# A two-layer CIN recommender tower on one core: the contraction goes by halves of a chunk's rows, as 64-column tiles, and the dense layers move to pairs 4 to 6

## The chip, the cores and the metric

The kernel runs on one core of one Trainium2 chip. The metric is the device time of one execution in microseconds; the median of several runs counts.

## What is computed

For each of 512 samples 32 rows of 64 numbers are gathered from 32 tables by index. Two layers of a compressed interaction network follow, then three dense layers. All is float32.

```python
def _cin_layer(X, prev_x, W, b):
    bsz, m, d = X.shape
    h = prev_x.shape[1]
    x_i = jnp.einsum('bmd,bhd->bmhd', X, prev_x).reshape(bsz, m * h, d)
    x_i = jnp.einsum('oc,bcd->bod', W, x_i) + b[None, :, None]
    return x_i
...
for W, b in ((W0, b0), (W1, b1)):
    x_i = _cin_layer(X, prev_x, W, b)
    cin_outs.append(x_i.sum(axis=2))
    prev_x = x_i
...
z = jnp.concatenate(cin_outs, axis=1)
h = jnp.concatenate([z, dense_ctx], axis=1)
h = jnp.maximum(h @ W_top1 + b_top1, 0.0)
h = jnp.maximum(h @ W_top2 + b_top2, 0.0)
y = h @ W_top3
```

W0 is 128 x 1024, W1 is 128 x 4096, W_top1 is 272 x 512, W_top2 is 512 x 256, W_top3 is 256 x 1.

## The kernel before

Only the sums of a layer's output over the 64 dimensions are wanted. So the kernel never forms the second layer: it computes, for each sample, the third-order moments of its fields (sum over d of x_i x_j x_m), and contracts them with coefficients that it first works out from W0 and W1.

**Setup.** W1 is multiplied with the pairs of W0 (L573, 64 matmuls), the results are folded and transposed (L595, 69 transposes), and the coefficients DT lie in the tile `coef`: 69 slots of 128 x 128. Eight more slots, W0Z, serve the first layer's output.

**Chunks.** The samples go in four chunks (c = 0 to 3) of 128. A chunk's rows are two halves h of 64 samples, one on partitions 0 to 63 and one on 64 to 127, where a partition is a dimension d. Sample numbers b within a half run from 0 to 63. A chunk has eight pairs (j = 0 to 7) of two steps each (k), and a step takes four values of b.

- *Gathers.* GpSimd gathers the rows of one field at a time (L269, 32 per chunk, eight to a group g) into XG. The gathers of group g of a chunk wait until TensorE has transposed that group of the chunk before.
- *x_group(c, g)* (L551): TensorE transposes eight fields, four transposes of 128 x 128 (L558). ScalarE and VectorE copy the result to XT, in the program order of each. Group 3 of the next chunk (its last) is transposed at the boundary between two chunks, the others behind pairs 1, 3 and 6 (chunk 0) or 1, 3 and 5.
- *products(c, j)* on VectorE (L370): PP, the products of two fields, for the eight values of b of a pair. ScalarE first copies XT to PSUM (x_copy) and fills two columns of PP (e_columns). PP has two buffers.
- *moments(c, k)* on TensorE (L598): 32 matmuls of 64 rows, 32 weight columns and 80 moving columns (L613). The trace shows a float32 matmul as two records, each a weight load (PEld) and a matmul (PE), so a step has 64 records and a pair 128. The outputs lie in two PSUM banks of the four 0 to 3.
- *moments_out(c, k)* on ScalarE (L480): one copy of 128 x 640 from those banks to U, which has two buffers, one for even and one for odd chunks. It adds one to the semaphore u_ev.
- *contract(c)* on TensorE (L618), a Python generator that emits one matmul, here called a tile, at each next(): 8 tiles with W0Z (L627), then 69 with DT (L632). The weights are 128 x 128, and the moving side is 128 columns of U, a whole chunk. They sum up in PSUM bank 6 as z0 and z1. It waits for u_ev of all sixteen steps of its chunk, and for z_ev, the eviction of the chunk before from bank 6. A chunk's 77 tiles are spread over the next chunk as filler between its moments: AHEAD tiles before the x_group at the boundary, BEHIND behind it, BETWEEN between the two steps of pair 0, and TILES[c][j] behind pair j. Chunk 3's stand alone at the end.
- *z_out(c)* on ScalarE (L491) evicts z0 and z1 to ZT in pair 5 of the next chunk. *layers* on TensorE (L659) and *layer_out* on ScalarE (L497) are the dense layers of the chunk before: h1 (L639, L644, L645) behind pair 6, h2 (L650) behind pair 7, y (L656) behind the boundary. They share banks 4 and 5 with the x_groups, in turns that `bank_uses` (L71) writes down.

Each engine works off its list in program order, and the order is written out by hand. The tables that set it on TensorE:

```python
XPAIR = ({1: 0, 3: 1, 6: 2}, {1: 0, 3: 1, 5: 2}, {1: 0, 3: 1, 5: 2}, {})
TILES = {1: (10, 6, 5, 5, 5, 5), 2: (14, 9, 9, 8, 8, 8), 3: (15, 9, 9, 9, 9, 9)}
AHEAD, BEHIND, BETWEEN = (26, 6, 2), 12, 3
LAYER = {6: "h1", 7: "h2"}
```

The loop over chunks and pairs stands at L679 and behind.

Of the kernel before, what the change touches and what calls it, by code (L numbers as in the profile page):

```python
# [18 lines left out]

# [1 line left out]

# [6 lines left out]
P = 128  # L30
NC = B // P
# [4 lines left out]
BW = HF + 4  # L36
# [3 lines left out]
TB = HF + 1  # L40
NT = NBK // NQ * TB
NN = NT + 1
BP = P // 2
KB = 4
NK = BP // KB
NJ = NK // 2
# [15 lines left out]
RESTS = (2, 4, 6)  # L62
WARM = 10
XPAIR = ({1: 0, 3: 1, 6: 2}, {1: 0, 3: 1, 5: 2}, {1: 0, 3: 1, 5: 2}, {})
TILES = {1: (10, 6, 5, 5, 5, 5), 2: (14, 9, 9, 8, 8, 8), 3: (15, 9, 9, 9, 9, 9)}
AHEAD, BEHIND, BETWEEN = (26, 6, 2), 12, 3
XFIELDS = F // NG
LAYER = {6: "h1", 7: "h2"}


def bank_uses():  # L71


    uses = [(("x", 0, g), 4 + g % 2) for g in range(NG)]
    later = []
    for c in range(NC):
        for j in range(NJ):
            if c and j in LAYER:
                later.append((LAYER[j], c - 1, 0))
            if j in XPAIR[c]:  # L80
                later.append(("x", c + 1, XPAIR[c][j]))
        if c < NC - 1:
            later.append(("x", c + 1, NG - 1))
        if c:
            later.append(("y", c - 1, 0))
    return uses + [(use, 4 + i % 2) for i, use in enumerate(later)]


def build(nc, ids, tables, near_a, near_b, cross_a, cross_b, w1t, w0z, b0, b1, ctxt, wt1, bt1, wt2, bt2, wt3, out):
# [3 lines left out]
    with ExitStack() as ctx:  # L93
        def sb(name, shape, dt=f32):
            return ctx.enter_context(nc.sbuf_tensor(name, shape, dt))
# [14 lines left out]
        U = main[:, U_AT:MAIN_N].rearrange("p (c n h b) -> p c n h b", c=2, h=2, b=BP)  # L110
# [9 lines left out]
        DT = coef[:, :].rearrange("p (n o) -> p n o", o=H)  # L120
# [9 lines left out]
        W0Z = sb("W0Z", [P, 8, H])  # L130
# [13 lines left out]
        bank = [psum[:, i, :] for i in range(8)]  # L144
# [21 lines left out]
        t_mm, u_ev = sem("t_mm"), sem("u_ev")  # L166
# [7 lines left out]
        for use, to in pair_uses:  # L174
            pair_bank[use] = to
            if use[0] == "x":
                _, c, g = use
# [235 lines left out]
        def _(act):  # L413
# [83 lines left out]
            def layer_out(c, layer):  # L497


                src = bank[pair_bank[layer, c, 0]]  # L500
                if layer == "h1":
                    act.wait_ge(h1_mm, 4 * (c + 1))
                    for k in range(4):
                        last = a.activation(H1[:, k, :], src[:, k * P:k * P + P], ACT.Relu, bias=bt1s[:, k:k + 1])
                elif layer == "h2":
                    act.wait_ge(h2_mm, 2 * (c + 1))
                    for n in range(2):
                        last = a.activation(H2[:, n, :], src[:, n * P:n * P + P], ACT.Relu, bias=bt2s[:, n:n + 1])
                else:
                    act.wait_ge(y_mm, c + 1)  # L510
                    last = copy(Y[:, P * c:P * c + P], src[0:1, 0:P])
                last.then_inc(pair_act, 1)

            for c in range(NC):
                for j in range(NJ):
                    moments_out(c, 2 * j)
                    moments_out(c, 2 * j + 1)
                    if j < NJ - 2:
                        x_copy(NJ * c + j + 2)
                        e_columns(NJ * c + j + 2)  # L520
                    if c and j in LAYER:
                        layer_out(c - 1, LAYER[j])
                    if c and j == 5:
                        z_out(c - 1)
                    if j in XPAIR[c]:
                        x_out(act, copy, c + 1, XPAIR[c][j], 0).then_inc(x_act, 1)
                if c < NC - 1:
                    last_group(c + 1)
                if c:
                    layer_out(c - 1, "y")  # L530
            z_out(NC - 1)

            for k in (0, 2):
# [9 lines left out]
        def _(pe):  # L543
            mm, transpose = nc.tensor.matmul, nc.tensor.transpose
# [39 lines left out]
            for i, n in enumerate(DORDER):  # L584
# [9 lines left out]
                for k in range(min(4, NN - 4 * n)):  # L594
                    last = transpose(bank[i % 4][:, k * P:(k + 1) * P], D[:, 4 * n + k].rearrange("p q m -> p (q m)"), ident[:, :])  # L595
# [19 lines left out]
                                      pp[:, :, q * 2 * BW:(q + 1) * 2 * BW], start=True, stop=True)  # L615
                last.then_inc(t_mm, 1)

            def contract(c):  # L618

                if c:  # L620
                    pe.wait_ge(z_ev, 2 * c)
                z1, z0 = bank[6][:, 0:P], bank[6][:, P:2 * P]
                pe.wait_ge(u_ev, NK * (c + 1))
                if c == 0:
                    pe.wait_ge(w0z_in, 16)
                for n in range(8):
                    mm(z0, W0Z[:, n, :], U[:, c % 2, n // 2 * BW + TB + n % 2].rearrange("p h b -> p (h b)"),  # L627
                       start=n == 0, stop=n == 7)
                    yield
                for n in range(NN):  # L630
                    at = n // TB * BW + n % TB if n < NT else BW - 1
                    last = mm(z1, DT[:, n, :], U[:, c % 2, at].rearrange("p h b -> p (h b)"), start=n == 0, stop=n == NN - 1)  # L632
                    if n == NN - 1:
                        last.then_inc(z_mm, 1)
                    yield

# [22 lines left out]
            def layers(c, layer):  # L659


                to = bank[pair_bank[layer, c, 0]]
                wait_out(pe, pair_before[layer, c, 0])
                if layer == "h1":
                    pe.wait_ge(z_ev, 2 * (c + 1))
                    pe.wait_ge(mlp_in, 64)
                    for k in range(4):
                        context(c, k, to[:, k * P:k * P + P])
                        layer_1(k, to[:, k * P:k * P + P])
                elif layer == "h2":  # L670
                    wait_out(pe, ("h1", c, 0))
                    for n in range(2):
                        layer_2(n, to[:, n * P:n * P + P])
                else:
                    wait_out(pe, ("h2", c, 0))
                    layer_3(to[0:1, 0:P])

            tiles = iter(())
            for c in range(NC):  # L679
                for j in range(NJ):  # L680
                    moments(c, 2 * j)
                    if c and j == 0:
                        for _ in range(BETWEEN):
                            next(tiles)
                    moments(c, 2 * j + 1)
                    for _ in range(TILES[c][j] if c and j < len(TILES[c]) else 0):
                        next(tiles)
                    if c and j in LAYER:
                        layers(c - 1, LAYER[j])
                    if j in XPAIR[c]:  # L690
                        x_group(c + 1, XPAIR[c][j])
                tiles = contract(c)
                if c < NC - 1:
                    for _ in range(AHEAD[c]):
                        next(tiles)
                if c < NC - 1:
                    x_group(c + 1, NG - 1)
                    for _ in range(BEHIND):
                        next(tiles)
                if c:  # L700
                    layers(c - 1, "y")
            for _ in tiles:
                pass

# [52 lines left out]
```

## Time and profile before

| what | us |
|---|---|
| median of three runs (363.14 to 365.93) | 365.27 |
| the profiled execution | 361.78 |
| its span, first to last instruction | 360.0 |
| TensorE matmuls busy | 260.7 |
| ScalarE / VectorE / GpSimd busy | 132.8 / 123.4 / 123.4 |
| mean granted TensorE clock, as a share of full speed | 0.796 |

Times within the execution count from the span's start. PE is TensorE's matmuls, PEld its weight loads, DVE VectorE, ACT ScalarE, POOL GpSimd. A row with "[0.93 <-issue]" says that the engine was idle for 0.93 us before it and that no wait seen in the trace explains it. "x18" counts records. The granted clock is given as a share of full speed, where 1.00 is 2.4 GHz and 0.50 is 1.2 GHz. In a merged row the time runs from the first record's start; some matmul records can be missing from a count.

### The profile page before, as it was taken

The numbers are of one execution on the slowest core, as the hardware profiler recorded it, in microseconds if no ns is written. First come the engines' busy times: TensorE is split into PE (matmuls) and PEld (weight loads), VectorE is DVE, ScalarE is ACT, GpSimd is POOL, SyncE is SP. The second block draws the span as 40 slices with busy tenths as digits, with TensorE's granted clock in tenths as the row PEclk, the third lists the DMA queues.
The fourth block names the chain that finished last, engine by engine and source line by source line (L and its number), as shares of the span: only waits on it lengthen the run. The fifth ranks groups of instructions, "written<-read, shape, count | busy, mean of one in ns | idle before, by whom it ended". The sixth has DMA issues, their size and how long they took to land.

```text
span 360.0 us, 11320 instructions
## 1 busy us (share of the span) xinstructions
PE 260.7 (72%) x5169; PEld 209.8 (58%) x5169; DVE 123.4 (34%) x243; ACT 132.8 (37%) x287; POOL 123.4 (34%) x134
## 2 busy tenths in 40 slices
PE   8654177957365647559594848768598999989997
PEld 7321055746142515348392727557397898978896
DVE  1000028282724334204351423306166728652001
ACT  4421156756432405203040403414055655645002
POOL 5777626377526270623507070524400000000000
PEclk9855559899558565859587765959699999999999
DMA  6911101011001010100101010000000000000000
GB/s 193 330 26 26 26 4 28 7 23 28 21 14 22 13 27 7 20 11 9 22 4 27 6 26 7 19 16 11 20 4 4 5 4 4 5 5 4 2 0 2
DMA packets 8657, 9.27 MB, mean 26 GB/s; under 512 B 4225, under 2 KB 5121, under 8 KB 8610
## 3 DMA queue, kind: packets, MB, share of 16 engines
q0 software_dynamic: 4096, 4.20, 5.8%
q1 hardware_dynamic: 3650, 4.34, 3.8%
q8 instruction: 41, 0.67, 0.8%
q10 hardware_dynamic: 864, 0.01, 0.1%
q14 instruction: 6, 0.05, 0.1%
HBM read 8.54 MB, written 0.00 MB: 24 GB/s over the span
## 4 chain that ended last, share of the span: by engine, by line
PE 69%; issue 20%; another core or an unknown queue 4%; ACT 4%; DVE 3%; POOL 0%; POOLq 0%; DVEq 0%; ACTq 0%
PE psum L613 24%; PE psum L632 20%; PE psum L573 11%; PE psum L627 3%; ACT main L417 2%; PE psum L650 2%; DVE PP L384 2%; PE psum L558 2%; PE psum L595 2%; PE psum L549 1%; PE psum L639 1%; PE psum L644 1%; PE psum L645 1%; ACT coef L417 1%
## 5 line engine op out<-in xcount | busy, mean ns | idle before, releaser
L269 POOL DMA_INDIRECT XG<-in_tbl,idx x128 | 122.7, 959 | 132.3 <-PE psum L558 90.3
L417 ACT ACTIVATE main<-psum 128x640 f32<-128x640 f32 (+4 forms) x146 | 80.0, 565 | 164.0 <-PE psum L613 96.2
L613 PE MATMUL psum<-PP,main 64*32 64x80 f32 x4096 | 95.3, 265 | 61.5 <-issue 52.9
L613 PEld LDWEIGHTS psum<-PP,main 64*32 64x32 f32 x4096 | 65.9, 118 | 87.3 <-issue 75.3
L384 DVE TENSOR_TENSOR PP<-psum,main 128x1024 f32<-128x1024 f32 (+1 forms) x72 | 76.2, 1101 | 90.5 <-ACT psum L417 90.1
L632 PE MATMUL psum<-main,coef 128*128 128x128 f32 x552 | 73.0, 290 | 1.9 <-issue 1.9
L632 PEld LDWEIGHTS psum<-main,coef 128*128 128x128 f32 x552 | 68.1, 202 | 7.1 <-issue 5.4
L573 PE MATMUL psum<-main 128*128 128x256 f32 (+1 forms) x128 | 42.9, 480 | 25.0 <-issue 16.3
L573 PEld LDWEIGHTS psum<-main 128*128 128x128 f32 x128 | 26.8, 227 | 40.1 <-issue 26.6
L417 ACT ACTIVATE coef<-psum 128x256 f32<-128x256 f32 (+2 forms) x43 | 20.3, 541 | 17.3 <-PE psum L573 7.6
L197 DVE COPY main<-psum 64x256 f32<-64x256 f32 (+1 forms) x26 | 9.3, 356 | 49.1 <-PE psum L558 45.2
L221 DVE COPY main<-psum 128x276 f32<-128x276 f32 x4 | 2.5, 631 | 41.6 <-remote 37.9
L317 DVE TENSOR_TENSOR main<-main,coef 128x128 f32<-128x128 f32 (+8 forms) x73 | 14.1, 263 | 3.4 <-issue 1.5
L417 ACT ACTIVATE PP<-main 128x256 f32<-128x256 f32 x32 | 14.7, 459 | 0.2
L417 ACT ACTIVATE psum<-main 128x256 f32<-128x256 f32 x32 | 12.3, 385 | 5.1 <-DVE PP L388 4.8
L388 DVE TENSOR_TENSOR PP<-psum,main 128x128 f32<-128x128 f32 (+1 forms) x36 | 13.8, 383 | 0.0
L595 PE MATMUL psum<-ident,main 128*128 128x128 f32 x69 | 8.8, 279 | 4.3 <-issue 2.0
L627 PE MATMUL psum<-main,W0Z 128*128 128x128 f32 x64 | 10.2, 319 | 2.0 <-ACT main L417 2.0
L558 PE MATMUL psum<-ident,XG 128*128 128x128 f32 x64 | 11.1, 302 | 0.0
L627 PEld LDWEIGHTS psum<-main,W0Z 128*128 128x128 f32 x64 | 9.5, 232 | 2.5 <-ACT main L417 2.3
L595 PEld LDWEIGHTS psum<-ident,main 128*128 128x128 f32 x69 | 7.4, 140 | 5.5 <-issue 2.7
L407 DVE TENSOR_SCALAR H<-psum,bt1s 128x128 f32<-128x128 f32 x2 | 0.7, 351 | 28.2 <-PE psum L645 28.2
(44 smaller groups left out, 95.8 us busy)
## 6 DMA issues: line engine op xcount, KB each, us to landing
main<-in_w1t SPq DMA_DIRECT2D x8, 256.0 KB
XG<-in_tbl,idx POOLq DMA_INDIRECT x128
WT<-in_wt SPq DMA_DIRECT2D x2, 512.0 KB
W0Z<-in_w0z SPq DMA_DIRECT2D x1, 512.0 KB
main<-in_near_a SPq DMA_DIRECT2D x1, 136.0 KB
main<-in_near_b SPq DMA_DIRECT2D x1, 136.0 KB
main<-in_cross_a SPq DMA_DIRECT2D x1, 128.0 KB
main<-in_cross_b SPq DMA_DIRECT2D x1, 128.0 KB
```

The lines of the kernel that those rows point to most:

```text
L197: last = copy(XT[rows, c % 2, b0:b1, at:at + XFIELDS - 1:2], src[:, BP * h + b0:BP * h + b1, :])
L269: pool.indirect_dma_start(out=XG[:, f, :], out_offset=None, in_=tables[f], in_offset=bass.IndirectOffsetOnAxis(ap=idx[:, c, f:f + 1], axis=0),
L317: last = v.tensor_tensor(d, d, in_fx(off, [[NX + HF, j1 - j0], [1, HF]]), ALU.add)
L384: v.tensor_tensor(pp[:, lo:lo + nb, g * NS:(g + 1) * NS, 0:HF], in_xp(lo * F + g * HF, [[F, nb], [0, NS], [1, HF]]), in_main(at, [[2 * XW, ...
L388: v.tensor_tensor(pp[:, lo:lo + nb, :, HF].rearrange("p b (g m) -> p b g m", g=2), XP[:, lo:lo + nb, :].rearrange("p b (g m) -> p b g m", ...
L417: return a.activation(dst, src, ACT.Copy)
L558: last = transpose(bank[pair_bank[use]][:, i * P:(i + 1) * P], XG[:, f:f + 2, :].rearrange("p f d -> p (f d)"), ident[:, :])
L573: mm(bank[n % 4][:, 0:pairs.shape[1]], W1T[:, m, :], pairs, start=True, stop=True).then_inc(v_mm, 1)
L595: last = transpose(bank[i % 4][:, k * P:(k + 1) * P], D[:, 4 * n + k].rearrange("p q m -> p (q m)"), ident[:, :])
L613: last = mm(bank[2 * (n % 2) + h][F * q:F * q + F, i * CW:i * CW + CW], XT[lo:lo + BP, c % 2, KB * k + i, NS:NS + F], pp[:, :, q * 2 * BW: ...
L627: mm(z0, W0Z[:, n, :], U[:, c % 2, n // 2 * BW + TB + n % 2].rearrange("p h b -> p (h b)"), start=n == 0, stop=n == 7)
L632: last = mm(z1, DT[:, n, :], U[:, c % 2, at].rearrange("p h b -> p (h b)"), start=n == 0, stop=n == NN - 1)
```

## The change

The contraction of a chunk goes by halves of the values of b. `contract(c, half)` takes as its moving side the 32 values of b of its half, in both h: 64 columns in place of 128, with the same weights. It writes the matching 64 columns of z0 and z1. Each half has its 77 tiles, and a chunk's two halves follow each other in one chain, which begins behind the moments of pair 4 (FROM) of the chunk itself. The first half waits for u_ev of eight steps, the second for all sixteen. Only the last tile of the second half signals z_mm.

The tables are new: TILES has an entry for all chunks and pairs, the x_group at a boundary has 26 tiles ahead of it after chunk 0 and none after chunks 1 and 2, and 24 behind it; 6 stand between the steps of pair 0. z_out moves from pair 5 to pair 3, h1 from 6 to 4, h2 from 7 to 5, and y from the boundary to pair 6, on TensorE and on ScalarE. Whatever of the chain is left after the last pair of chunk 3 is emitted at the end as before.

```diff
@@ -62,10 +63,12 @@
 RESTS = (2, 4, 6)
 WARM = 10
 XPAIR = ({1: 0, 3: 1, 6: 2}, {1: 0, 3: 1, 5: 2}, {1: 0, 3: 1, 5: 2}, {})
-TILES = {1: (10, 6, 5, 5, 5, 5), 2: (14, 9, 9, 8, 8, 8), 3: (15, 9, 9, 9, 9, 9)}
-AHEAD, BEHIND, BETWEEN = (26, 6, 2), 12, 3
+FROM = NJ // 2
+TILES = ((0, 0, 0, 0, 19, 19, 19, 20), (12, 3, 3, 3, 10, 12, 17, 19),
+         (20, 16, 15, 15, 10, 12, 17, 19), (20, 16, 15, 15, 19, 19, 19, 20))
+AHEAD, BEHIND, BETWEEN = (26, 0, 0), 24, 6
 XFIELDS = F // NG
-LAYER = {6: "h1", 7: "h2"}
+LAYER = {4: "h1", 5: "h2", 6: "y"}
 
 
 def bank_uses():
@@ -81,8 +84,6 @@
                 later.append(("x", c + 1, XPAIR[c][j]))
         if c < NC - 1:
             later.append(("x", c + 1, NG - 1))
-        if c:
-            later.append(("y", c - 1, 0))
     return uses + [(use, 4 + i % 2) for i, use in enumerate(later)]
 
 
@@ -520,14 +521,12 @@
                         e_columns(NJ * c + j + 2)
                     if c and j in LAYER:
                         layer_out(c - 1, LAYER[j])
-                    if c and j == 5:
+                    if c and j == FROM - 1:
                         z_out(c - 1)
                     if j in XPAIR[c]:
                         x_out(act, copy, c + 1, XPAIR[c][j], 0).then_inc(x_act, 1)
                 if c < NC - 1:
                     last_group(c + 1)
-                if c:
-                    layer_out(c - 1, "y")
             z_out(NC - 1)
 
             for k in (0, 2):
@@ -615,22 +614,22 @@
                                       pp[:, :, q * 2 * BW:(q + 1) * 2 * BW], start=True, stop=True)
                 last.then_inc(t_mm, 1)
 
-            def contract(c):
-
-                if c:
+            def contract(c, half):
+
+                if c and half == 0:
                     pe.wait_ge(z_ev, 2 * c)
-                z1, z0 = bank[6][:, 0:P], bank[6][:, P:2 * P]
-                pe.wait_ge(u_ev, NK * (c + 1))
-                if c == 0:
+                rows = slice(half * BP // 2, (half + 1) * BP // 2)
+                z1, z0 = [bank[6][:, at:at + P].rearrange("p (h b) -> p h b", h=2)[:, :, rows] for at in (0, P)]
+                pe.wait_ge(u_ev, NK * c + NK // 2 * (half + 1))
+                if c == 0 and half == 0:
                     pe.wait_ge(w0z_in, 16)
                 for n in range(8):
-                    mm(z0, W0Z[:, n, :], U[:, c % 2, n // 2 * BW + TB + n % 2].rearrange("p h b -> p (h b)"),
-                       start=n == 0, stop=n == 7)
+                    mm(z0, W0Z[:, n, :], U[:, c % 2, n // 2 * BW + TB + n % 2, :, rows], start=n == 0, stop=n == 7)
                     yield
                 for n in range(NN):
                     at = n // TB * BW + n % TB if n < NT else BW - 1
-                    last = mm(z1, DT[:, n, :], U[:, c % 2, at].rearrange("p h b -> p (h b)"), start=n == 0, stop=n == NN - 1)
-                    if n == NN - 1:
+                    last = mm(z1, DT[:, n, :], U[:, c % 2, at, :, rows], start=n == 0, stop=n == NN - 1)
+                    if half and n == NN - 1:
                         last.then_inc(z_mm, 1)
                     yield
 
@@ -675,7 +674,6 @@
                     wait_out(pe, ("h2", c, 0))
                     layer_3(to[0:1, 0:P])
 
-            tiles = iter(())
             for c in range(NC):
                 for j in range(NJ):
                     moments(c, 2 * j)
@@ -683,22 +681,20 @@
                         for _ in range(BETWEEN):
                             next(tiles)
                     moments(c, 2 * j + 1)
-                    for _ in range(TILES[c][j] if c and j < len(TILES[c]) else 0):
+                    if j == FROM:
+                        tiles = itertools.chain(contract(c, 0), contract(c, 1))
+                    for _ in range(TILES[c][j]):
                         next(tiles)
                     if c and j in LAYER:
                         layers(c - 1, LAYER[j])
                     if j in XPAIR[c]:
                         x_group(c + 1, XPAIR[c][j])
-                tiles = contract(c)
                 if c < NC - 1:
                     for _ in range(AHEAD[c]):
                         next(tiles)
-                if c < NC - 1:
                     x_group(c + 1, NG - 1)
                     for _ in range(BEHIND):
                         next(tiles)
-                if c:
-                    layers(c - 1, "y")
             for _ in tiles:
                 pass
```

TensorE, chunk 0 from pair 4 to pair 0 of chunk 1. L613 is moments (64 matmuls a pair), L627 and L632 the tiles, L558 an x_group. Before:

```order
L613 MATMUL psum<-PP,main 32x80 x192
L558 MATMUL psum<-ident,XG 128x128 x4
L613 MATMUL psum<-PP,main 32x80 x64
L627 MATMUL psum<-main,W0Z 128x128 x8
L632 MATMUL psum<-main,coef 128x128 x18
L558 MATMUL psum<-ident,XG 128x128 x4
L632 MATMUL psum<-main,coef 128x128 x12
L613 MATMUL psum<-PP,main 32x80 x32
L632 MATMUL psum<-main,coef 128x128 x3
```

The same stretch now, where the lines are one or more lower (L612 moments, L631 the tiles with DT, L557 an x_group):

```order
L612 MATMUL psum<-PP,main 32x80 x64
L627 MATMUL psum<-main,W0Z 128x2x32 x8
L631 MATMUL psum<-main,coef 128x2x32 x11
L612 MATMUL psum<-PP,main 32x80 x64
L631 MATMUL psum<-main,coef 128x2x32 x19
L612 MATMUL psum<-PP,main 32x80 x64
L631 MATMUL psum<-main,coef 128x2x32 x19
L557 MATMUL psum<-ident,XG 128x128 x4
L612 MATMUL psum<-PP,main 32x80 x64
L631 MATMUL psum<-main,coef 128x2x32 x20
L627 MATMUL psum<-main,W0Z 128x2x32 x8
L631 MATMUL psum<-main,coef 128x2x32 x18
```

The first half's 77 tiles stand in pairs 4 to 7 of chunk 0 itself, and the 26 behind them belong to the second half.

TensorE at the end of chunk 3, from the moments of pair 7 on. Before (L650 is h2 and L656 y of chunk 2, L639 the first matmuls of chunk 3's h1):

```order
L613 MATMUL psum<-PP,main 32x80 x64
L650 MATMUL psum<-H,WT 128x128 x8
L656 MATMUL psum<-H,wt3s 1x128 x2
L627 MATMUL psum<-main,W0Z 128x128 x8
L632 MATMUL psum<-main,coef 128x128 x69
L639 MATMUL psum<-CTX,WT1C 128x128 x4
```

Now, from the tiles of pair 5 on (L649 is h2, L655 y, L638 the context part of h1):

```order
L631 MATMUL psum<-main,coef 128x2x32 x19
L649 MATMUL psum<-H,WT 128x128 x8
L612 MATMUL psum<-PP,main 32x80 x64
L631 MATMUL psum<-main,coef 128x2x32 x19
L655 MATMUL psum<-H,wt3s 1x128 x2
L612 MATMUL psum<-PP,main 32x80 x64
L631 MATMUL psum<-main,coef 128x2x32 x20
L627 MATMUL psum<-main,W0Z 128x2x32 x8
L631 MATMUL psum<-main,coef 128x2x32 x69
L638 MATMUL psum<-CTX,WT1C 128x128 x4
```

The end still has 77 tiles, now of half the columns; h2 and y have left it.

## Rows read from the trace of the kernel before

**Rows 1.** The page: engine, busy us, share, records; and the chain by engine

```profile
PE 260.7 (72%) x5169; PEld 209.8 (58%) x5169; DVE 123.4 (34%) x243; ACT 132.8 (37%) x287; POOL 123.4 (34%) x134
...
PE 69%; issue 20%; another core or an unknown queue 4%; ACT 4%; DVE 3%; POOL 0%; POOLq 0%; DVEq 0%; ACTq 0%
```

**Rows 2.** Windows: us, busy us (records) by engine, clock, DMA share, GB/s

```profile
126.84:136.90 10.06, 4.48 (x36) 1.99 (x36) 2.63 (x5) 0.01 (x1) 6.57 (x7) 0.56 0.15 28
136.90:144.18 7.28, 5.67 (x298) 5.03 (x298) 4.47 (x5) 4.83 (x9) 0.00 (x0) 0.50 0.02 5
158.40:166.25 7.85, 7.85 (x54) 7.85 (x55) 0.00 (x0) 0.00 (x0) 0.00 (x0) 0.76 0.00 0
218.55:225.22 6.67, 6.67 (x160) 6.06 (x167) 3.42 (x4) 3.83 (x9) 0.00 (x0) 0.62 0.01 2
258.26:292.12 33.86, 32.56 (x1115) 29.59 (x1115) 18.68 (x24) 18.18 (x39) 0.00 (x0) 0.96 0.02 4
298.21:331.67 33.46, 31.66 (x1174) 29.03 (x1175) 19.91 (x24) 16.72 (x36) 0.00 (x0) 1.00 0.02 4
305.93:309.66 3.73, 3.73 (x147) 3.49 (x147) 2.61 (x3) 2.00 (x4) 0.00 (x0) 1.00 0.03 7
337.11:352.52 15.41, 15.41 (x140) 15.41 (x140) 0.00 (x0) 0.00 (x0) 0.00 (x0) 1.00 0.00 1
```

**Rows 3.** GpSimd and TensorE in chunk 0, timelines: start, us, what, [idle before]

```profile
125.55 0.94 POOL L269 DMA_INDIRECT XG<-in_tbl,idx  x1 [6.73 <-PE psum L558]
...
129.76 0.49 PE L613 MATMUL psum<-PP,main 64*32 64x80 f32 x4 [0.93 <-issue]
...
136.90 3.34 PE L613 MATMUL psum<-PP,main 64*32 64x80 f32 x170 [0.23 <-issue]
141.84 2.41 PE L613 MATMUL psum<-PP,main 64*32 64x80 f32 x128 [1.60 <-DVE PP L388]
```

**Rows 4.** The chain in chunk 3, one pair: start, us, what

```profile
305.93 2.21 PE psum L632 x18
308.13 1.53 PE psum L613 x115
```

**Rows 5.** The chain behind the last moments: start, us, what

```profile
333.76 0.63 ACT H L508 x2
...
334.53 0.60 PE psum L656 x4
335.12 1.98 PE psum L627 x16
337.11 15.41 PE psum L632 x138
```

**Rows 6.** Weight loads singly (start, us), then by line (duration ns min/median/max)

```profile
331.67 0.19 PEld L650 LDWEIGHTS psum<-H,WT 128*128 128x128 f32 x1
331.67 0.30 PEld L650 LDWEIGHTS psum<-H,WT 128*128 128x128 f32 x2
...
357.51 0.09 PEld L656 LDWEIGHTS psum<-H,wt3s 128*1 128x1 f32 x2 [0.64 <-DVE H L409]
...
L650 PEld LDWEIGHTS psum<-H,WT x10: 186/192/192, 331.7 to 332.7; 128*128 128x128 f32 x10
L650 PE MATMUL psum<-H,WT x9: 275/275/377, 331.7 to 332.7; 128*128 128x128 f32 x9
...
L656 PEld LDWEIGHTS psum<-H,wt3s x4: 79/82/83, 357.5 to 357.7; 128*1 128x1 f32 x4
...
L613 PEld LDWEIGHTS psum<-PP,main x721: 102/106/108, 305.0 to 330.0; 64*32 64x32 f32 x181
```

**Rows 7.** The warm-up matmuls, L549: in the chain, and durations in ns

```profile
1.52 4.22 PE psum L549 x20
...
L549 PEld LDWEIGHTS psum<-ident x20: 192/333/338, 1.5 to 5.4; 128*128 128x128 f32 x20
```

**Rows 8.** TensorE's timeline where chunk 0's contraction begins

```profile
158.40 1.01 PE L627 MATMUL psum<-main,W0Z 128*128 128x128 f32 x3 [1.96 <-ACT main L417]
```

More of the change, by code:

```diff
@@ L22 @@
+import itertools
 from contextlib import ExitStack
```

## Prediction

> **What bounds the kernel now.** I read the engine rows and the chain first. TensorE is busy for 72% of the span, and the chain that ended last is 69% TensorE with 20% "issue" [rows 1]. So the end is set by what TensorE executes, and by stretches in which it gets no instructions.
>
> The windows by stage show two regimes [rows 2]. While GpSimd sends the eight gathers of a group, TensorE is nearly empty: 36 matmul records in 10.06 us (126.84:136.90), then 298 in 7.28 us as soon as the gathers end. Inside stand rows of four records of L613 behind 0.93 us of "issue", again and again; this one reaches from the first gather at 125.55 to 136.90, 11.3 us [rows 3]. Such a slow stretch stands behind each x_group as long as there are gathers (to 257 us), and its end hangs on the gathers' time, not on what TensorE has to do. The other regime is chunks 2 and 3: TensorE is busy 32.56 of 33.86 us and 31.66 of 33.46 us, at full clock [rows 2]. A pair there takes 3.73 us: 2.21 for nine tiles (18 records) and 1.53 for its 128 moments records [rows 4], while VectorE works 2.61 and ScalarE 2.00 us [rows 2]. TensorE bounds these chunks and every tile added is paid. At the end, one chunk's whole contraction stands alone: 15.41 us of L632 behind 1.98 us of L627, and before it layer 3 waits 0.8 us for ScalarE [rows 5].
>
> **Price of a tile of 64 columns.** This decides. A float32 matmul is two records, each a weight load and a matmul. 138 records take 15.41 us, 0.1117 us each, so an old tile costs 0.2235 us at full clock [rows 5]. The new tile moves half the columns, but its weights are the same 128 x 128, loaded again for each half. What does such a load cost? At 331.67 the array had just run out, and two loads of L650 follow each other: one takes 0.19 us, the two together 0.30 us, so the second began 0.11 us behind the first. The first matmul took 377 ns where the median is 275: it waited some 102 ns for its weights [rows 6]. With one weight column two loads fit into 0.09 us together [rows 6]. Over the widths a load takes 79 to 83 ns (1 column), 102 to 108 (32), 186 to 192 (128): 107 ns more for 127 columns more [rows 6]. So a load of 128 columns occupies its path for 107 to 109 ns. It is hidden today, with 3 to 5 ns to spare, under matmuls of 128 moving columns; under 64 columns (half of 111.7, 56 ns) it is not. Bounds of the half tile: 0.112 us (half the old one: loads cost nothing) and 0.2235 us (nothing saved). I take two loads of 0.109, 0.218 us, the value of the row that shows the load itself. At half clock 20 records take 4.22 us and the load 333 ns in place of 192 [rows 7], so either kind of tile costs 0.42 us there.
>
> The contraction goes from 308 tiles to 616. At 0.218 this is 134 us of TensorE where it was 69.
>
> **The change by stages.** Tiles before and after, from the tables and the order:
> (a) chunk 0 and the boundary behind it: 38, then 127. (b) chunk 1 with its boundary: 57, then 109. (c) chunk 2, boundary, chunk 3: 136, then 303. (d) the end: 77 and 77.
>
> (a) Pairs 4 to 6 get 57 half tiles where none stood. The slow stretch ends at 136.90 and the clock is at half until beyond 144 [rows 2]; as TensorE is now filled without a break I take 4 us at half clock: 10 tiles by 0.42 and 47 by 0.218, 14.4 us. Taken off: 1.6 us of waiting for VectorE, which the tiles fill [rows 3], and 0.7 us for each of pairs 5 and 6, whose 128 moments records take 1.72 us at full clock (3.73 less 18 x 0.1117) and not 2.41 [rows 3, 4]. Net +11.4. Pair 7 is slow as before, then come 20 tiles, the first 12 at half clock: 6.7 us, less the 2.0 us for which the contraction waited for ScalarE [rows 8]; the next 26 take 5.7 where 26 old ones took 7.85, partly at half clock [rows 2]. Net +2.5. Behind the x_group stand 24 tiles, not 12; they lie in the next slow stretch, whose end doesn't move, and only push 24 moments records out of it, 0.02 us each: +0.5. Sum +14.4.
>
> (b) Up to the x_group of pair 1 there are 2 more (+0.6); to that of pair 3, 4 fewer, at half clock (-1.7); to that of pair 5, 12 more; to that of the end, 30 more. These 42 extend catch-up stretches in which the clock has had time to rise (mean 0.62 over the 6.67 us from 218.55 [rows 2]): 42 x 0.218 = 9.1. Behind the x_group 12 more: +0.5. Sum +8.5.
>
> (c) 303 x 0.218 less 136 x 0.2235 is +35.7. Idle time of TensorE is 1.3 and 1.8 us [rows 2]; as part of it is "issue", tiles fill half: -1.5. Sum +34.2.
>
> (d) 77 x 0.0055 is -0.4. Layer 3 of chunk 2 has left for pair 6; the 1.4 us from 333.74 to 335.12 go [rows 5]. The contraction's wait for the last moments lies behind 20 tiles, in chunk 3 as in chunk 0. What is late next is the load stream itself, so the end stays about 17 us. Sum -1.8.
>
> Costed at nothing: the dense layers, the same matmuls at other pairs. Their evictions run on ScalarE, which has 1.7 us free per pair and more now. The new contraction waits for z's eviction in pair 4; that eviction (two short operations of ScalarE) has pair 4's 128 moments records for cover, at least 1.72 us. Without the cover the first tile would wait, and with it the next pair's moments, queued behind, and ScalarE and VectorE that take them up: under 1 us by my estimate (half of the 2.0 us in rows 8, which hold a larger eviction), three times. The banks alternate by the new order and each use before lies a pair or more back.
>
> Together 14.4 + 8.5 + 34.2 - 1.8 = +55.3 us. The profiled execution took 361.78 us (span 360.0 and 1.8 around it), so 417.1 by its own time. The runs' median, 365.27, lies 3.5 above it: forecast 420.6.
>
> **Rivals.** *Half price.* The half tile costs 0.112 us: the loads of a matmul stream hide whatever the moving width. For it: the load of 32 columns in the moments costs no 26 ns, since 128 records pass in 1.72 us, 13 ns each. Against it: those loads go to different parts of the array, the tiles' to the whole of it, and the 0.11 us of rows 6 were seen with nothing else running. By stage: (a) 20 tiles at 0.21 and 37 at 0.112, less 3.0, then 4.2 less 2.0, then 2.9 for 7.85: +2.6 with rounding; (b) 12.2 for 12.7: -0.5; (c) 33.9 for 30.4, less 1.5: +2.0; (d) 8.6 for 17.4 and layer 3: -10.2. Sum -6.1: 359.2, faster by 1.7%. It decides for the other side once a half tile costs less than some 0.12 us.
>
> The Trainium skill (TensorE: Matmul & The Clock Gate, Back-to-back issue gap) gives the gap of an isolated matmul as its columns over 2.4 GHz plus 2.5 ns, and adds that in a stream with weight loads both set the spacing. The first alone would make two passes of 64 columns 58 ns a record, the rival's 359 to 362; the gap of 111.7 ns agrees with it at 128 columns, and no row here shows 64.
>
> *Partly hidden.* Loads of one tile overlap partly, 0.165 us: halfway, +24.6, 390. For it only that no row has a load longer than its matmul.
>
> *Low clock.* Taking weights rather than moving columns, TensorE keeps the half clock in (a) and (b): 55 and 42 tiles at 0.42, +20 us, 440. For it: the clock was 0.50 through 7.28 us of catching up. Against it: it was 1.00 in the 15.41 us of tiles [rows 2].
>
> **Chances.** Forecast 0.78, low clock 0.08, partly hidden 0.05, half price 0.09. The range 398 to 438 leaves out half price, partly hidden and the upper half of low clock. The likeliest's own range is 0.214 to 0.2235 a tile with 6 us for the clock. Faster by over 1% 0.08, within 1% 0.04 (about what a measurement of this kernel can tell from no change), slower by over 1% 0.88.
>
> **What would show it.** In the profile after: records of the new tiles 0.107 to 0.112 us apart at full clock, weight loads busy almost without a gap, L631 near 15.4 us at the end, chunk-3 pairs of 5 us and more (15 tiles: 1.72 + 3.3). Records 0.056 to 0.06 us apart and an end under 10 us would prove me wrong. If the tiles are at 0.109 but the total is off, look at the granted clock in chunks 0 and 1.

## The result and the profile after

The changed kernel takes 445.7 us (median of four runs, 445.04 to 446.0), the kernel before 365.26 us beside it. The ratio is 1.221, with a 95% interval from 1.216 to 1.226. The sign was forecast, the size was not: 420.6 us was forecast, 398 to 438 was the range, and the measured time lies 7.7 us above its upper end. The medians are 80.4 us apart; the spans of the two profiled executions are 83.6 apart (443.6 and 360.0), since the one of the kernel before was 3.5 us quicker than its median. The stages and sums of the forecast are compared on spans.

The page of the changed kernel, in the parts that answer to [rows 1], with the tiles' group:

```profile
PE 358.1 (81%) x5785; PEld 310.4 (70%) x5785; DVE 123.3 (28%) x243; ACT 131.5 (30%) x287; POOL 122.6 (28%) x134
...
PEclk9755599965765795555587579655599999999999
...
PE 77%; issue 13%; another core or an unknown queue 5%; ACT 3%; DVE 2%; POOL 0%; POOLq 0%; DVEq 0%; ACTq 0%
...
L631 PE MATMUL psum<-main,coef 128*128 128x64 f32 x1104 | 164.0, 319 | 0.0
L631 PEld LDWEIGHTS psum<-main,coef 128*128 128x128 f32 x1104 | 159.5, 233 | 4.3 <-issue 2.6
```

TensorE's matmuls are busy 97 us more, and the tiles alone 104 us: 164.0 us of L631 and 23.0 of L627 stand where L632 and L627 had 73.0 and 10.2. PEclk, the granted clock over 40 slices, stands at 5 (half clock) through several slices at a time, also in the middle of the kernel, where the contraction runs.

**The price.** The chain in the last chunk and at the end, answering to [rows 4, 5]:

```profile
389.45 1.53 PE psum L612 x114
390.98 1.93 PE psum L627 x16
...
418.98 1.79 PE psum L627 x16
420.77 15.41 PE psum L631 x138
```

The 138 records of the end take 15.41 us, as they did with twice the columns. The durations of single records there (ns, min/median/max):

```profile
L631 PE MATMUL psum<-main,coef x127: 275/275/275, 420.8 to 434.9; 128*128 128x64 f32 x127
L631 PEld LDWEIGHTS psum<-main,coef x127: 192/192/192, 420.9 to 435.0; 128*128 128x128 f32 x127
```

Loads of 192 ns and matmuls of 275 ns are the numbers of a matmul with 128 moving columns in [rows 6]. The records stand 111.7 ns apart, not the 58 ns or less of the rival "half price". A tile of 64 columns costs 0.2235 us at full clock, the upper bound of the forecast and 0.0055 above the value taken.

**The clock.** Windows of the changed kernel, with the columns of [rows 2]:

```profile
140.19:148.49 8.30, 8.30 (x46) 8.18 (x54) 2.68 (x3) 1.36 (x3) 0.00 (x0) 0.50 0.00 0
183.21:194.30 11.09, 11.09 (x53) 11.09 (x54) 0.00 (x0) 0.00 (x0) 0.00 (x0) 0.50 0.01 1
195.15:205.29 10.14, 10.14 (x57) 10.02 (x63) 6.58 (x13) 3.40 (x10) 7.23 (x8) 0.50 0.11 20
282.86:302.14 19.28, 19.28 (x98) 19.16 (x105) 6.58 (x13) 4.11 (x11) 7.23 (x8) 0.50 0.06 11
305.02:317.77 12.75, 12.75 (x124) 12.29 (x131) 2.68 (x3) 2.06 (x4) 0.00 (x0) 0.50 0.00 1
420.77:436.18 15.41, 15.41 (x139) 15.41 (x139) 0.00 (x0) 0.00 (x0) 0.00 (x0) 1.00 0.00 1
```

From 183.21 to 194.30 TensorE is busy without a gap, with nothing but tiles, and the clock stays at 0.50 (1.2 GHz). With the 40 tile records before (from 174.48 in the chain), the x_group at 194.30 and the 48 tile records behind it, this dense stretch reaches from 174.48 to 205.29: 30.8 us at half clock. The same holds for the 19.28 us from 282.86, which are tiles and one x_group too. At the end the same kind of tiles runs at 1.00 (2.4 GHz) throughout. How many tile records ran at half clock is counted by windows over the stretches of half clock, with L631's instructions alone, then with L627's (us, PE busy (records), PEld busy (records), clock, DMA share, GB/s):

```profile
129.87:150.35 20.48, 4.90 (x22) 4.81 (x22) 0.50 0.06 13
167.42:222.03 54.61, 36.77 (x166) 35.95 (x166) 0.50 0.05 9
228.86:239.10 10.24, 2.16 (x9) 1.98 (x10) 0.50 0.07 14
245.93:259.58 13.65, 1.06 (x4) 0.97 (x4) 0.50 0.07 13
280.06:321.02 40.96, 27.83 (x127) 27.39 (x127) 0.50 0.05 9
```

```profile
129.87:150.35 20.48, 3.67 (x16) 3.49 (x16) 0.50 0.06 13
167.42:222.03 54.61, 3.62 (x16) 3.53 (x16) 0.50 0.05 9
245.93:259.58 13.65, 3.67 (x16) 3.48 (x16) 0.50 0.07 13
280.06:321.02 40.96, 3.88 (x16) 3.61 (x16) 0.50 0.05 9
```

That is 328 records of L631 and 64 of L627, 392 of 1232. Counted in the same way the kernel before has 60 of 616. By the stages of the forecast it is 179 in (a), 157 in (b) and 56 in (c), where the kernel before has 18, 36 and 6.

**Where the 83.6 us of span went.** The stages of the forecast, each read as the distance between the same two places of both chains:

| stage | forecast | measured |
|---|---|---|
| setup, to the first moments (94.17, then 97.14) | 0 | +3.0 |
| (a) to the first tile between the steps of pair 0, chunk 1 (177.75, then 208.12) | +14.4 | +27.4 |
| (b) to the same place in chunk 2 (258.26, then 305.02) | +8.5 | +16.4 |
| (c) to the last contraction, without layer 3's stay (333.74, then 418.98) | +34.2 | +38.5 |
| (d) that stay and the end | -1.8 | -1.6 |

### The profile page after: what moved, and what is told of

It reads as the page before. It is cut to its first block, busy times and chain, and to the rows that moved or that the text cites. A ratio compares the mean times of both kernels' runs of the same rounds, so it can differ in the third digit from the quotient of the medians.

```text
span 443.6 us, 12551 instructions
## 1 busy us (share of the span) xinstructions
PE 358.1 (81%) x5785; PEld 310.4 (70%) x5785; DVE 123.3 (28%) x243; ACT 131.5 (30%) x287; POOL 122.6 (28%) x134
## 4 chain that ended last, share of the span: by engine, by line
PE 77%; issue 13%; another core or an unknown queue 5%; ACT 3%; DVE 2%; POOL 0%; POOLq 0%; DVEq 0%; ACTq 0%
PE psum L631 36%; PE psum L612 19%; PE psum L572 8%; PE psum L627 5%; ACT main L418 2%; PE psum L557 2%; DVE PP L385 1%; PE psum L649 1%; PE psum L594 1%; PE psum L548 1%; PE psum L638 1%; PE psum L643 1%; PE psum L644 1%; ACT coef L418 1%
## 5 line engine op out<-in xcount | busy, mean ns | idle before, releaser
L631 PE MATMUL psum<-main,coef 128*128 128x64 f32 x1104 | 164.0, 319 | 0.0
L631 PEld LDWEIGHTS psum<-main,coef 128*128 128x128 f32 x1104 | 159.5, 233 | 4.3 <-issue 2.6
L612 PE MATMUL psum<-PP,main 64*32 64x80 f32 x4096 | 90.5, 268 | 47.3 <-issue 44.1
L612 PEld LDWEIGHTS psum<-PP,main 64*32 64x32 f32 x4096 | 63.3, 119 | 71.3 <-issue 64.5
L572 PEld LDWEIGHTS psum<-main 128*128 128x128 f32 x128 | 27.4, 230 | 41.2 <-issue 30.3
L627 PE MATMUL psum<-main,W0Z 128*128 128x64 f32 x128 | 23.0, 350 | 0.0
L627 PEld LDWEIGHTS psum<-main,W0Z 128*128 128x128 f32 x128 | 21.7, 261 | 1.0 <-issue 0.4
L557 PE MATMUL psum<-ident,XG 128*128 128x128 f32 x64 | 11.7, 313 | 0.0
```

What stands on the lines that cost most here:

```text
L557: last = transpose(bank[pair_bank[use]][:, i * P:(i + 1) * P], XG[:, f:f + 2, :].rearrange("p f d -> p (f d)"), ident[:, :])
L572: mm(bank[n % 4][:, 0:pairs.shape[1]], W1T[:, m, :], pairs, start=True, stop=True).then_inc(v_mm, 1)
L612: last = mm(bank[2 * (n % 2) + h][F * q:F * q + F, i * CW:i * CW + CW], XT[lo:lo + BP, c % 2, KB * k + i, NS:NS + F], pp[:, :, q * 2 * BW: ...
L627: mm(z0, W0Z[:, n, :], U[:, c % 2, n // 2 * BW + TB + n % 2, :, rows], start=n == 0, stop=n == 7)
L631: last = mm(z1, DT[:, n, :], U[:, c % 2, at, :, rows], start=n == 0, stop=n == NN - 1)
```

## The experiments

The times of a kernel differ a great deal between chips: the kernel before takes 365 to 370 us on some and 235 to 237 us on others (medians; below). So every ratio here is to the kernel before on the same chip. The times are medians of six runs (e4, e5), four (e7, e11), one (w1, w2) or two (all others). Where an expectation gives a time in us, it was written for a chip on which the kernel before takes 365 us; e1 to e4 ran where it takes 369.7.

### e1: the split alone

```diff
-                for n in range(8):
-                    mm(z0, W0Z[:, n, :], ...)
+                for i in range(2 * (8 + NN)):
+                    half, n = divmod(i, 8 + NN)
+                    rows = slice(half * BP // 2, (half + 1) * BP // 2)
...
+                    if i % 2:
                         yield
```

Order, tables and dense layers are those of the kernel before; where one tile stood, two of 64 columns stand.

> The kernel before, in its own order, but each tile of 128 columns is emitted as two of 64 columns. Theory A (a half tile is bound by its two weight loads, 0.11 us each, and a stream of half tiles doesn't bring the granted clock up to full speed): records 0.1117 us apart at full clock, the contraction at the end about 34.4 us in place of 17.4, total 440 to 460 us. Theory B (the price doubles, but the half clock came from the new places of the tiles): 425 to 435 us, share of tile records at half clock near that of the kernel before (10%). Theory C (the split costs little, the new places cost it): 365 to 385 us.

Measured: 459.0 us, 1.241 times the kernel before (1.231 to 1.251), which took 369.7 us there. The chain at the end:

```profile
414.63 1.93 PE psum L631 x16
416.56 15.41 PE psum L636 x138
431.97 1.79 PE psum L631 x16
433.76 15.41 PE psum L636 x138
```

It is the whole contraction twice, 34.5 us for what took 17.4. Of the 1232 tile records 377 ran at half clock, 172 of them in one stretch of 58 us (L636 alone):

```profile
155.89:213.91 58.02, 37.47 (x172) 37.13 (x172) 0.50 0.04 8
```

Theory C is out: the loss comes without any of the new places. Theory B is out too: the half clock comes with the split. The new places gave a little back (1.22 and not 1.24). They keep half of the work from the end, which fits; that this is the reason wasn't tested.

### e2: wide tiles in the second half

```diff
-                rows = slice(half * BP // 2, (half + 1) * BP // 2)
+                rows = slice(0, BP if half else BP // 2)
```

> The changed kernel, where only the second half's tiles move all 128 columns again, so that they repeat the first half's work. Theory A: a tile costs the same two loads, 0.2235 us at full clock, 138 records at the end in 15.4 us as before; the wide tiles bring the clock up, so fewer tile records run at half clock and the total falls to 415 to 435 us although TensorE does half as much arithmetic again. Theory B (the half clock comes from the places, not the width): 445 us within 1%. Theory D (64 columns do cost less than 128 somewhere): over 450 us.

Measured: 437.2 us beside 369.7, ratio 1.182 (1.171 to 1.193), under the changed kernel's 1.216 to 1.226. The end again, and the tile records at half clock (L631 alone):

```profile
415.00:430.42 15.42, 15.42 (x141) 15.42 (x140) 0.00 (x0) 0.00 (x0) 0.00 (x0) 1.00 0.00 1
```

```profile
133.38:164.10 30.72, 14.83 (x68) 14.55 (x68) 0.50 0.04 7
174.34:191.40 17.06, 8.79 (x40) 8.61 (x40) 0.50 0.05 10
205.06:215.30 10.24, 4.22 (x18) 3.93 (x19) 0.50 0.06 11
276.74:307.46 30.72, 18.06 (x82) 17.81 (x82) 0.50 0.07 13
```

The time fell although TensorE computes the first half twice. The total lies 2 us above the band expected; the direction is A's. The price of a tile is the same at the end (15.42 us), and 218 records of L631 ran at half clock here (208 in these rows, 10 in two short stretches), where the changed kernel has 328. The 110 fewer by 0.101 us (0.213 less 0.1117) are 11 us; the ratio's difference is 0.039 of 369.7, 14 us.

### e3: half the weight columns

```diff
+                    w = P if n in (0, NN - 1) else P // 2
-                    last = mm(z1, DT[:, n, :], ...)
+                    last = mm(z1[0:w], DT[:, n, 0:w], ...)
```

The same for W0Z. Half of z's outputs is left out, except for what the first and last tile of each sum add.

> The changed kernel, where a tile loads only 64 of the 128 weight columns, except for the first and last of each sum (4 of 77); the other half of z's outputs is left out. Theory A: loads fall to 0.053 to 0.056 us, records of the end 0.056 to 0.06 us apart, L631 there about 8 to 9 us in place of 15.41, total 345 to 375 us. Rival E (each record has a fixed cost of 0.11 us for its instructions): 15.4 us at the end and 445 us within 1%.

Measured: 387.0 us, 1.046 times the kernel before (1.037 to 1.055). The end, and single records there (ns):

```profile
369.08 1.43 PE psum L628 x16
370.51 8.55 PE psum L633 x138
```

```profile
L633 PE MATMUL psum<-main,coef x124: 222/222/222, 371.3 to 378.5; 128*64 128x64 f32 x124
L633 PEld LDWEIGHTS psum<-main,coef x121: 138/138/138, 371.4 to 378.4; 128*64 128x64 f32 x121
```

138 records take 8.55 us, 62 ns each, and loads 138 ns in place of 192. Nothing but the weight columns differs, so the load was the bound, and Rival E's fixed cost per record is out. The total missed its band by 12 us. My rival "half price" had 359 us for nearly this case, and even so the new order is slower than the old one. Two things are part of it. The records of both lines cost somewhat more than half (0.062 and 0.089 us each), so that the whole contraction at full clock comes to some 80 us by my estimate (1104 and 128 records) and not 69. And 191 of the 1232 tile records ran at half clock: more than the 60 of the kernel before, but half of the changed kernel's 392, with the same moving columns and the same places. How the rest divides was not taken apart.

### e4: whole tiles at the early places

```diff
-TILES = {1: (10, 6, 5, 5, 5, 5), 2: (14, 9, 9, 8, 8, 8), 3: (15, 9, 9, 9, 9, 9)}
+TILES = {1: (12, 8, 8, 8), 2: (20, 12, 12, 12), 3: (21, 13, 13, 13)}
-LAYER = {6: "h1", 7: "h2"}
+LAYER = {4: "h1", 5: "h2", 6: "y"}
```

z_out goes to pair 3 with them.

> The kernel before with whole tiles, but its contraction is done by pair 3 (12, 8, 8, 8 tiles and so on behind pairs 0 to 3), z is evicted in pair 3 and the dense layers stand in pairs 4 to 6, as in the changed kernel. Theory A: these moves cost nothing and layer 3's wait at the end (1.4 us) goes, 361 to 366 us. Theory C (the places of the dense layers and of the tiles carry the loss): over 370 us.

Measured: 374.7 us beside 369.7, ratio 1.012 (1.005 to 1.018). In the chain the 1.4 us that layer 3 gave up went to another wait: the last contraction now waits for ScalarE to copy the last moments.

```profile
345.96 1.39 ACT main L415 x2
347.35 0.14 issue
347.49 2.02 PE psum L623 x16
```

The 361 to 366 us hoped for didn't come. The time in us even lies in the band of Theory C (over 370), but there the kernel before itself takes 369.7. By the ratio the moves cost about 1%, not the 22% of the change, so Theory C is out as the cause of the loss; why it is 1% slower was not settled.

### w1 and w2: one stream of matmuls, two widths

```diff
-WARM = 10
+WARM = 100
-                mm(bank[7][:, 0:P], ident[:, :], ident[:, :], start=True, stop=True)
+                mm(bank[7][:, 0:64], ident[:, :], ident[:, 0:64], start=True, stop=True)
```

w2 keeps 0:P.

> The kernel before with 100 warm-up matmuls (200 records) in place of 10, moving 64 columns of the identity, one behind the other from 1.5 us on. Theory A: the granted clock stays at 0.50 through all of them, records 0.213 us apart (a load of 128 weight columns at half clock), 42 to 43 us in all. Rival F (the clock rises with any unbroken stream of matmuls, whatever its columns): full clock within 10 us, records then 0.107 to 0.112 us apart, 25 us in all.

> The same 100 warm-up matmuls, moving 128 columns. Theory A and F alike: the clock rises within 10 us, records 0.1117 us apart from then on, 24 to 27 us in all. If the clock stays low here too, the warm-up place says nothing about width.

The chain of w1 at the start, and its loads (ns):

```profile
1.52 42.93 PE psum L549 x200
44.45 14.10 PE psum L573 x52
```

```profile
L549 PEld LDWEIGHTS psum<-ident x200: 286/333/333, 1.5 to 43.9; 128*128 128x128 f32 x100
```

The same of w2:

```profile
1.52 24.54 PE psum L549 x200
26.06 11.57 PE psum L573 x52
```

```profile
L549 PEld LDWEIGHTS psum<-ident x200: 192/192/333, 1.5 to 25.7; 128*128 128x128 f32 x100
```

200 records of 64 columns take 42.93 us, 0.215 each: half clock from the first to the last. 200 records of 128 columns take 24.54 us, and the median load falls from 333 to 192 ns: the clock rose. Half the moving columns, and the stream takes 1.75 times as long. Rival F is out. The granted clock of these first stretches is told here by the distance of the records and by the loads' durations. The trace's first entry of the clock is full clock from 49.33 us in w1 and from 5.62 us in w2; for the time before it has none, and a window there reads 1.00 all the same. So w1's clock rose 4.9 us behind the last of the 64-column records, among the wider matmuls of L573, whose 52 records take 14.10 us there and 11.57 in w2.

### e6, e8, e9, e12: chips without slow stretches

The changed kernel and the kernel of e2 ran again on other chips.

> The changed kernel once more, beside the kernel before on the same chip. On a chip with slow stretches: 1.20 to 1.24 times the kernel before. On one without (the kernel before at 235 us there): Theory A, 77 to 85 us of added time if the half clock comes back with the half tiles, 60 to 69 us if without gathers' idle stretches the clock stays full (308 tiles more by 0.2235 us is 68.8).

> The changed kernel, as the partner of the next run. 1.26 times the kernel before on a chip without slow stretches, 1.20 to 1.24 times on one with them.

> The kernel of e2. Theory A on a chip without slow stretches: there is next to no half clock to win back and a tile of 64 columns costs what one of 128 costs, so within 1% of e8. On a chip with them: 2.5 to 4.5% faster than e8. Theory D (wide tiles cost more than the narrow ones at full clock): 9 us or more slower than e8 (308 tiles by 0.03 us).

> The kernel of e2. On a chip with slow stretches Theory A 1.17 to 1.19 times the kernel before, as in e2, and under the 1.22 of the changed kernel; on one without 1.24 to 1.27 times, the same as the changed kernel there (1.26).

| run | us | the kernel before there |
|---|---|---|
| e6, changed | 298.5 (298.1, 298.9) | 236.6 |
| e8, changed | 293.6 (290.5, 296.8) | 235.7 |
| e9, second half wide | 297.3 (294.1, 300.5) | 235.7, with e8 |
| e12, second half wide | 300.6 (298.1, 303.1) | 236.9, the chip of e6 |

The engines' busy times of e6 (span 297.0 us) and its stages (boundary 0/1 and chunk 1; chunk 2 to the end of chunk 3; the last contraction):

```profile
PE 279.4 (94%) x5785; PEld 258.8 (87%) x5785; DVE 123.4 (42%) x243; ACT 128.9 (43%) x287; POOL 122.7 (41%) x134
```

```profile
92.43:158.37 65.94, 63.07 (x1529) 58.08 (x1527) 26.14 (x39) 25.28 (x57) 46.53 (x50) 0.97 0.14 28
158.37:272.37 114.00, 113.30 (x2812) 108.59 (x2810) 47.93 (x68) 43.98 (x100) 7.77 (x8) 1.00 0.03 6
272.37:289.56 17.19, 17.19 (x155) 17.19 (x155) 0.00 (x0) 0.00 (x0) 0.00 (x0) 1.00 0.00 1
```

The clock is 0.97 and 1.00, and in the whole execution 47 of 1232 tile records ran at half clock. The added time is 61.9 us (298.5 less 236.6), a little under the 68.8 us of 308 tiles by 0.2235. This is the price nearly by itself. Wide and narrow tiles in the second half are told apart by the quicker run of each: 294.1 and 290.5 us on one chip, 1.2% (the 1% expected for e9 was just missed), and 298.1 both on the other. So wide tiles gain nothing where there is next to no half clock to win back, as A has it, and the 9 us of Theory D are not there. Differences of 1% are not resolved by these runs.

### e5, e7, e10, e11: tiles into the slow stretches

```diff
-TILES = {1: (10, 6, 5, 5, 5, 5), 2: (14, 9, 9, 8, 8, 8), 3: (15, 9, 9, 9, 9, 9)}
-AHEAD, BEHIND, BETWEEN = (26, 6, 2), 12, 3
+TILES = {1: (0, 12, 0, 12), 2: (14, 9, 9, 9, 9), 3: (14, 9, 9, 9, 9)}
+AHEAD, BEHIND, BETWEEN = (26, 0, 0), 24, 3
...
+                    if c == 1 and j in XPAIR[c]:
+                        x_group(c + 1, XPAIR[c][j])
...
-                    if j in XPAIR[c]:
+                    if c != 1 and j in XPAIR[c]:
```

The x_groups of chunk 1 move ahead of their pair's tiles.

> The kernel before with whole tiles, where they stand right behind an x_group, in the slow stretch of the gathers, and not in the catch-up behind it: 24 behind each boundary, 12 behind the x_groups of pairs 1 and 3 of chunk 1, none elsewhere in chunk 1. Theory G (a slow stretch lets through a fixed number of records in a fixed time, so long records in it are free; this is where the part of the added tiles went that the changed kernel's time doesn't show): on a chip with slow stretches 8 to 14 us faster than the kernel before; on one without them within 1%. Rival H (tiles in a slow stretch lengthen it by their own time): no change within 1%, or slower where the later chunks carry more tiles.

> The same kernel as in e5, to see it on a chip with slow stretches. If this chip has them (the kernel before near 365 to 370 us): Theory G 8 to 14 us faster than the kernel before, Rival H no change within 1% or slower. If it has none (235 us): 1.02 times the kernel before, as in e5.

> The kernel of e5. On a chip with slow stretches Theory G 8 to 14 us faster than the kernel before, Rival H no change within 1% or slower; on one without 1.02 times the kernel before.

> The kernel of e5 once more. On a chip with slow stretches (the kernel before near 365 to 370 us) Theory G 8 to 14 us faster than the kernel before, Rival H no change within 1% or slower; on one without 1.02 times the kernel before.

All four came to chips without slow stretches: 242.5, 242.0, 241.2 and 242.0 us, ratios 1.024, 1.020, 1.023 and 1.018 (intervals within 1.008 to 1.030). The first one's "within 1%" was missed. Whether the order gains where there are slow stretches stays open, and no kernel here beat the kernel before.

What speaks for Theory G stands in two rows, from the end of the boundary's x_group to the tile between the steps of pair 0: the kernel before, then the changed one.

```profile
166.68:177.75 11.07, 6.51 (x90) 4.52 (x88) 6.58 (x13) 3.44 (x10) 7.78 (x8) 0.76 0.11 21
```

```profile
195.15:208.12 12.97, 12.02 (x114) 11.35 (x112) 6.58 (x13) 3.40 (x10) 7.77 (x8) 0.50 0.11 20
```

Both hold one group of gathers and 64 moments records. The changed kernel has 24 tile records more there, 5.1 us by 0.213, and all its 48 at half clock (10.13 us for them, against 2.68 us for 24 before), and yet the stretch is only 1.9 us longer. It is argued from one pair of rows, not shown by an experiment.

## Why the prediction missed

**What held.** The bound named (TensorE executes, every tile added is paid), the mechanism (a load of 128 columns isn't hidden under 64 moving columns) and its source, two loads 0.11 us apart, held: e3 and the unchanged 15.41 us show it. The end took 17.2 us (17.4 before); (d) was right within 0.2 us. On a chip without slow stretches 62 us of the 68.8 show (e6).

**The step that failed** is the clock in (a) and (b): "as TensorE is now filled without a break I take 4 us at half clock", and 42 tiles of (b) at full clock since the clock "has had time to rise". I took busy time for what raises the clock. The half clock lasted from 129.87 to 150.35, then from 167.42 to 222.03, and again from 280.06 to 321.02. Each of these stretches begins in a slow stretch and goes on through dense half tiles. In the chain of the changed kernel, where two of them end:

```profile
148.49 2.19 PE psum L612 x128
...
317.77 2.34 PE psum L612 x128
320.11 4.17 PE psum L631 x32
```

The rise at 150.35 falls among 128 moments records, that at 321.02 comes just behind another 128. Those at 222.03 and 239.10 come 2.2 and 0.6 us behind 128 more, and that at 259.58 among the matmuls of h1. None of the five stands behind more than 1 us of tiles alone. w1 and w2 show it by themselves: a stream of 64-column matmuls that began at half clock stayed there for its 42.93 us, and in one of 128 columns it rose. Begun at full clock, 34.5 us of half tiles kept it in e1. So where the clock fell in a slow stretch, it didn't come back while half tiles alone followed. In (c), at full clock in the forecast from end to end, 56 tile records still ran at half clock.

**The sizes, on spans.** Tile records at half clock: 392, where the kernel before has 60. The 332 more by 0.101 us are 33.6 us. The price is 308 by 0.2235, 68.8 us. With the setup's 3.0 these make 105.4; the span grew by 83.6. So some 22 us were taken in by waits and slow stretches. These 22 us are a remainder, and no run shows them by themselves. The forecast had 65.5 for the price, some 4 for half clock, and 14 taken in. The clock's term was too small by 30 us, and too little was let go against it by 8.

**The rival "low clock"** had the mechanism and nearly the size: 440 us for 97 more tiles at half clock; 166 more than before it became, and 445.7 us. That its time came so near is in part luck: its clock term was 10 us too small, and so were the price and the setup by 3 each, while 8 us too little was taken off. It had 0.08, since the clock was 1.00 in the 15.41 us at the end [rows 2]. That row showed that tiles keep the clock, whole ones at that; it doesn't show that half tiles raise it. The 0.50 through 7.28 us of catching up [rows 2] was the nearer witness, though of moments and not of half tiles. "Half price" and "partly hidden" are out. The range should have reached past "low clock" and not to its middle, for up to the start of chunk 2 every x_group brings a slow stretch, and with it a chance for the clock to fall.

**The setup** was costed at nothing and took 3.0 us more, with the same instructions in it. Other kernels begin their moments at other times too (98.55 in e4), and the profiled execution of the kernel before was 3.5 us quicker than its median, so this may be no more than the spread between executions. No run settles it.

## What to carry to other kernels

Halving the moving side of a float32 matmul with 128 weight columns, from 128 to 64, saved nothing here, since its weight load is then the longer part; look in the trace for two loads that follow each other with an empty array, and compare with the records' distance in a dense stream. Splitting a contraction to begin it early then pays for the early start with the whole of its price again. And where a kernel drops to half clock now and then, count what kind of matmul follows: TensorE busy without a gap was no sign here that the clock would come back.

## What the runs showed of the hardware that was not expected

**A stream can be dense and stay at half clock.** 200 records of 64 columns: 42.93 us, loads of 333 ns throughout; 200 of 128 columns: 24.54 us.

**Slow stretches came with the chip, not with the kernel.** The same kernel before took 363 to 366 us beside the changed kernel, 369.7 on the chip of e1 to e4, and 235.3 to 239.0 on four others. The gathers last as long there (0.94 us each), but TensorE isn't starved while they run: e6's TensorE is busy 63.07 of 65.94 us, 46.53 us of gathers beside it, and its moments begin at 49.4 us and not at 97.1. What differs between the chips the profile doesn't show, nor whether it is the chip or its state at the time. The size of a change need not carry over: the changed kernel costs 80 us more on the one kind and 58 to 62 on the other, and is slower on both.
